# A four-layer vision kernel on one core: the next image's last quarter in the place of the gates' indicators, and letters of their own for setup and tail

## The chip, the core and the metric

The kernel runs on one core of one Trainium2 chip. A core has five engines with instruction streams of their own: TensorE (PE; PEld is its weight load), VectorE (DVE), ScalarE (ACT), GpSimd (POOL) and SyncE (SP), which here only issues DMAs. The metric is the device time in microseconds (us), the median of several runs. Times of single instructions come from one profiled execution.

## The reference

The input x is 8 images of 256 channels and 64 x 64 pixels in float32. Four layers follow each other, each as x + f(groupnorm(x)) with 32 groups:

```
layer 0: b1 = x * sigmoid(bn(conv7x7(max, mean of x over H)))  # maps over (channel, column)
         b2 = the same over W (channel, row); b3 = the same over channels (row, column)
         wts = softmax over the three branches of conv1d(channel means of (b1 + b2 + b3) / 3)
         out = wts[0]*b1 + wts[1]*b2 + wts[2]*b3
layer 1: w = a[0]*weight + sum_i a[i+1] * circulant(weight, b), b = 2, 4, 8, 16; a = softmax(alphas)
         out = conv3x3(x, w)
layer 2: out = x * sigmoid(W2 relu(W1 mean(dwt_ll(x))))          # squeeze and excitation
layer 3: windows of 8 x 8, shifted by 4; qkv = x @ w_qkv + b; 8 heads of 32
         out = softmax(q k^T / sqrt(32) + bias + mask) v @ w_o + b_o
```

## The kernel before, in words

An image has 2 tiles of 128 channels (t or co) by 4096 pixels, held in X. A unit is a half image of one tile, 128 x 2048 values (1 MB); units 0 to 3 go by half, then tile. Layers 0 to 2 are the "front" of an image, in named steps: norm0a to c, reduce0 to 15, zpool, hwconv to hwmean7 (the three gates' maps), logits, mix, mixturn, gate0 to 17, norm1a to c, lift0 to 3 (the first rows of the Winograd form of the convolution), conv0.0 to conv23.1, convend. Each unit's result after layer 2 is stored to scratch_x in DRAM. Layer 3 works on window rows, 64 in all (8 per image), one image behind the front, reading scratch_x.

The order on each engine is written out by hand. The front is the "main line" (letter M); everything else is a stream with a letter. FIRST says which letters are executed after which step of image 0, TURN the same for each later image, AHEAD where they may run ahead, LAST_ROWS the letters after the last front. `play` walks main line and letters and takes the next piece of a stream for each letter. Engines execute in this order and wait on semaphores. The letters that matter here are, on SP, L (load a window row) and S (store it); on POOL, R (row and column sums of the next image), D and W (convolution and DWT work), N (the normalisation of the softmax, L856), O (the lower halves of the heads' output); on ACT, K (tokens), Q (evacuations of a filled bank), X (exponentials, L1129, eight instructions of 64 columns for a unit of 512 scores), T (turned probabilities, L1136), O (heads); on DVE, C (group statistics of the next image, L1615), U (its maxima, L1630), V (row sums for the DWT), J (joined rows), S (bias and maximum, L1724 and L1735), T (totals), A (addition of the attention); on PE, Q (fills: products for q, k, v and the output), S (scores), T (turns), W (weighings with the values).

All fills go through one PSUM bank, QP. A fill waits until the one before it has been read.

The setup (circulant weights, their Winograd halves, the scaling of w_qkv and w_o, the bias tables) stands on the main line: load, alpha and bands ahead of image 0, and the rest after the steps that SETUP_AT names. ScalarE issues sixteen DMAs for w_conv before its first computation.

The next image arrives in X during the convolution: unit u is fetched when its x2 is stored and the DWT has used it, so the fourth is fetched after convend. The gates of layer 0 need, for each pixel, a value that depends on its column and one that depends on its row, both by channel. They are made by TensorE as ab (the values, 64 columns and 64 rows on the 128 partitions) times `ind`, 128 x 4096 indicators of 0 and 1 (L185 and following). `ind` lies behind the tables of the 7 x 7 filters in l0c, and since the convolution uses all of l0c for its waves, tables and indicators are loaded again for every image.

## Time and profile before

| | us |
|---|---|
| median of 3 runs (lowest, highest) | 2962.48 (2961.73, 2963.66) |
| the profiled execution | 2961.15 |
| its span in the profile | 2959.0 |
| image 0 up to its convolution's end | 379.3 |
| its boundary to the first transposes of image 1 | 63.6 |
| a steady image (image 5, 1715.7 to 2043.3) | 327.6 |
| the last eight window rows (from 2698.8) | 260.2 |

The stretches are cut where the last matmul of a convolution ends. Busy time is of the engine alone, and an engine that is busy is not always what the others wait for. PEclk is the granted clock of TensorE as a share of full speed.

### The profile page before, as it was taken

The numbers are of one execution on the slowest core, as the hardware profiler recorded it, in microseconds if no ns is written. First come the engines' busy times: TensorE is split into PE (matmuls) and PEld (weight loads), VectorE is DVE, ScalarE is ACT, GpSimd is POOL, SyncE is SP. The second block draws the span as 40 slices with busy tenths as digits, with TensorE's granted clock in tenths as the row PEclk, the third lists the DMA queues.
The fourth block names the chain that finished last, engine by engine and source line by source line (L and its number), as shares of the span: only waits on it lengthen the run. The fifth ranks groups of instructions, "written<-read, shape, count | busy, mean of one in ns | idle before, by whom it ended". The sixth has DMA issues, their size and how long they took to land.

```text
span 2959.0 us, 68446 instructions
## 1 busy us (share of the span) xinstructions
PE 2369.5 (80%) x27236; PEld 1319.3 (45%) x27236; DVE 2293.1 (77%) x4555; ACT 1707.6 (58%) x4440; POOL 1383.2 (47%) x1052
## 2 busy tenths in 40 slices
PE   0157728899698978899798978898898979898776
PEld 0132315544454545444454545444544545454443
DVE  6868675878787887878887887888887888886443
ACT  0231118655766558654875567654876567655776
POOL 4304471365724574455634573356534572364222
PEclk9977859999899989999899989999999989999998
DMA  5400040004110240005100330005010421011101
GB/s 157 118 3 10 34 149 16 30 30 150 60 37 23 80 143 30 30 30 167 49 31 23 116 107 31 30 30 186 31 44 21 139 72 45 23 51 58 44 30 37
DMA packets 91347, 184.51 MB, mean 62 GB/s; under 512 B 37510, under 2 KB 50454, under 8 KB 80406
## 3 DMA queue, kind: packets, MB, share of 16 engines
q1 hardware_dynamic: 88854, 177.78, 18.5%
q8 instruction: 216, 3.54, 0.5%
q10 hardware_dynamic: 2176, 2.36, 0.3%
q14 instruction: 101, 0.83, 0.1%
HBM read 107.23 MB, written 72.86 MB: 61 GB/s over the span
## 4 chain that ended last, share of the span: by engine, by line
PE 52%; DVE 22%; ACT 11%; issue 7%; POOL 5%; ACTq 1%; SPq 0%; DMA 0%; DVEq 0%; POOLq 0%
PE F L1950 21%; PE QP L2006 6%; PE QP L2022 4%; PE QP L2013 4%; PE SP L2038 3%; PE O L2066 2%; ACT xs L1129 2%; PE PTR L2048 2%; PE F L1828 2%; PE F L1852 1%; ACT g_raw L1011 1%; DVE Z L1630 1%; DVE xs L1748 1%; ACT tmp L968 1%; ACTq L927 1%
## 5 line engine op out<-in xcount | busy, mean ns | idle before, releaser
L1950 PE MATMUL F<-g_raw,cw_hi 128*128 128x512 f16 x2304 | 701.6, 387 | 35.9 <-ACT tmp L1000 23.3
L856 POOL TENSOR_TENSOR xs<-xs,rec 128x512 f32<-128x512 f32 x256 | 283.2, 1107 | 754.2 <-DVE rec L1740 752.3
L1129 ACT ACTIVATE xs<-xs,mx 128x64 f32<-128x64 f32 x2048 | 511.3, 336 | 89.0 <-DVE mx L1735 88.9
L1950 PE MATMUL F<-g_raw,cw_lo 128*128 128x512 f16 x1152 | 443.9, 385 | 0.0
L1950 PEld LDWEIGHTS F<-g_raw,cw_hi 128*128 128x128 f16 x2304 | 220.8, 99 | 293.9 <-ACT tmp L1000 26.9
L1724 DVE TENSOR_TENSOR xs<-SP,bias 128x512 f32<-128x512 f32 (+2 forms) x384 | 181.6, 500 | 112.4 <-PE SP L2038 111.2
L841 POOL TENSOR_TENSOR tmp<-X,uw 128x512 f32<-128x512 f32 x128 | 175.6, 1384 | 186.2 <-DVE X L1587 172.2
L2006 PE MATMUL QP<-tok_hi,qkv_hi 128*128 128x512 f16 x512 | 199.1, 389 | 75.8 <-ACT qq L1114 24.1
L1739 DVE TENSOR_REDUCE sums<-xs 128x8 f32<-128x512 f32 x256 | 173.5, 678 | 94.9 <-ACT xs L1129 93.9
L1852 PE MATMUL F<-ident,g_raw 128*128 128x128 f32 x512 | 102.7, 318 | 156.1 <-ACT tmp L968 143.4
L1327 DVE SCALAR_TENSOR_TENSOR g_raw<-l0c,gn,g_raw 128x512 f16<-128x512 f32 x192 | 177.1, 967 | 52.2 <-ACT g_raw L990 36.3
L865 POOL TENSOR_TENSOR ot_lo<-ot,ot_hi 128x512 f16<-128x512 f32 x128 | 151.9, 1207 | 115.2 <-ACT ot_hi L1150 102.0
L1136 ACT ACTIVATE prt<-PTR 128x512 f32<-128x512 f32 x256 | 150.4, 587 | 90.3 <-PE PTR L2048 89.4
L1630 DVE TENSOR_REDUCE Z<-X 128x16 f32<-128x1024 f32 x128 | 197.7, 1556 | 2.8 <-DMA X<-in_x 2.8
L2006 PE MATMUL QP<-tok_lo,qkv_hi 128*128 128x512 f16 x512 | 197.2, 385 | 0.0
L2006 PE MATMUL QP<-tok_hi,qkv_lo 128*128 128x512 f16 x512 | 197.1, 385 | 0.0
L1748 DVE SCALAR_TENSOR_TENSOR xs<-QP,wm,xs 128x480 f32<-128x480 f32 (+1 forms) x256 | 111.7, 478 | 97.3 <-PE QP L2022 96.8
L2066 PE MATMUL O<-prt,vv 64*32 64x64 f32 x8192 | 167.4, 222 | 23.1 <-ACT prt L1136 22.3
L1117 ACT ACTIVATE kk<-QP,bq,gm 128x512 f32<-128x512 f32 x128 | 99.4, 777 | 148.3 <-PE QP L2006 148.3
L1735 DVE TENSOR_REDUCE mx<-xs 128x8 f32<-128x512 f32 x256 | 175.7, 686 | 8.8
L1114 ACT ACTIVATE qq<-QP,q_bias,q_scale 128x512 f32<-128x512 f32 x128 | 99.3, 776 | 141.5 <-PE QP L2006 141.5
L2048 PE MATMUL PTR<-ident,xs 128*128 128x128 f32 x1024 | 166.3, 287 | 16.5 <-POOL xs L856 12.3
(288 smaller groups left out, 5652.1 us busy)
## 6 DMA issues: line engine op xcount, KB each, us to landing
X<-in_x SPq DMA_DIRECT2D x32, 1024.0 KB, 6.2
scratch_x<-X SPq DMA_DIRECT2D x32, 1024.0 KB, 5.2
xs<-scratch_x SPq DMA_DIRECT2D x56, 512.0 KB, 3.6
out_x<-xs SPq DMA_DIRECT2D x56, 512.0 KB, 2.7
l0c<-scratch_t SPq DMA_DIRECT2D x8, 1876.0 KB, 10.5
l0c<-in_c_ind SPq DMA_DIRECT2D x8, 1024.0 KB, 6.3
l0c<-scratch_t SPq DMA_DIRECT2D x8, 640.0 KB, 12.7
l0c<-scratch_t SPq DMA_DIRECT2D x8, 576.0 KB, 13.2
```

The costliest lines, as they stand in the source:

```text
L841: G.tensor_tensor(rows_view(tmp[:, 2 + m % 2, :]), rows_view(X[:, co, lo:lo + CHUNK]), uw[:, :].unsqueeze(1).to_broadcast([P, ROWS, W]), A ...
L856: G.tensor_tensor(keyed(sc[:, u % 4, :]), keyed(sc[:, u % 4, :]), rec[:, u % 4, :].unsqueeze(2).to_broadcast([P, 8, TOK]), ALU.mult).then_ ...
L1129: last = S.activation(keys, keys, ACT.Exp, bias=mx[:, u % 4, i:i + 1])
L1327: V.scalar_tensor_tensor(vin[:, slot(half, comp), 1, t, :, 1:1 + W], rows_view(src[:, t, :]), g_r[:, t:t + 1], vin[:, slot(half, comp), 0, ...
L1630: V.tensor_reduce(Zv[:, t, kind, 0, PAD + W // 4 * i:PAD + W // 4 * (i + 1)], view[:, part, :], AX.X, ALU.max).then_inc(max_set, 1)
L1724: return V.tensor_tensor(sc[:, buf, :].rearrange("p (g w m) -> p g w m", g=CT, w=4)[:, :, span, :], SP[:, hs, :].rearrange("p (g w m) -> p ...
L1735: V.tensor_reduce(mx[:, buf, :], keyed(sc[:, buf, :]), AX.X, ALU.max, negate=True).then_inc(s_max, 1)
L1739: seq.link(V.tensor_reduce(sums[:, u % 4, :], keyed(sc[:, u % 4, :]), AX.X, ALU.add))
L1950: last = T.matmul(F[:, n % 2, :], wgt[:, ci, C3 * comp + dx, P * co:P * co + P], win[which], start=(ci == 0 and dx == 0 and j == 0), stop= ...
L2006: last = T.matmul(QP[:, :], wgt[:, ci, P * oc:P * oc + P], tk[:, ci, :], start=(j == 0), stop=(j == 5))
L2048: last = T.transpose(PTR[:, P * b:P * b + P], sc[:, u % 4, P * b:P * b + P], ident[:, :])
L2066: last = T.matmul(O[DH * (h % 4):DH * (h % 4) + DH, par, cols:cols + TOK], vv[rows, pair, DH * h:DH * h + DH], prt[rows, u % 2, P * b + TO ...
```

## The change

- **Gates.** `ind` is replaced by `eyes`, two identities of 64 columns one above the other (128 x 64). ab is computed twice, on both halves of the partitions, so that the upper half carries the high halves of the float16 split and the lower half the remainders. A chunk of eight rows takes three matmuls as before; the column part reads `eyes` broadcast over rows, the row part reads eight of its columns, each broadcast over 64. Four transposes instead of two bring ab into place.
- **Early quarter.** The 8 KB per partition that are free in l0c are `quad`: unit 3 of the next image is fetched there as soon as the waves of the convolution have been used (v_lo). The other three go to X as before. `given` tells each reader where a unit lies. Units arrive in the order 0, 3, 1, 2, and statistics and maxima are taken in this order. Gate step 9 writes image data into the place of unit 3 in X, and waits for its store and its use.
- **Maxima and sums by halves.** Column maxima are taken for each half and joined by one instruction. GpSimd's sums over rows are split in halves for their first three additions.
- **Setup.** It has the letter Y on each engine, with more and smaller pieces. w_conv is loaded by SP with eight DMAs of 16 partitions; the circulant weights are stored with eight instead of sixteen.
- **SyncE.** Stores of x2, fetches and constants are the letters Z, F and G.
- **Tail.** In the last eight window rows fills go round three banks, QP and the two of F. Values are taken out of the bank by DVE (P). POOL subtracts the maxima from a unit of scores (X, a 128 x 512 addition) and ACT takes one exponential over 512 columns.
- All tables of letters are other ones, and so is where every stream stands.

```diff
 FIRST = {
-    "SP": {"convend": "L"},
+    "SP": {"reduce0": "Y", "reduce11": "Y", "hwgate": "Y", "band1": "Z", "band2": "YF", "hwmean3": "Z",
+        "conv10.0": "G", "conv13.0": "F", "conv14.0": "F", "conv15.0": "Z", "conv22.1": "F", "convend": "ZL"},
...
 LAST_ROWS = {
-    "POOL": "ENONNNONNNNONNNNNONNNNONNNNNONNNNONNNONNNNNONNO",
+    "POOL": "ENEONNNNXOXNXNXNXNNXONXNXNXXNONXNXXNXNXONXNNXXNXXNONNXXNONXNXNXXNOXNNXXNXNXOXNNNO",
...
-        ind = l0c[:, n_toep + n_hw + n_1d:].bitcast(fp16)
+        quad = l0c[:, n_toep + n_hw + n_1d:]
...
+        def given(img, t, half):
+
+            if img and (half, t) == (1, CT - 1):
+                return quad
+            return X[:, t, HW // 2 * half:HW // 2 * half + HW // 2]
+
+        ARRIVAL = (0, 3, 1, 2)
...
+        ENDING = ROWS_ALL - NW
+        ALONE = FILL[f"q0.{ENDING}"]
+        BY_DVE = [name for name in FILLS if name[0] == "p" or name[0] == "v" and int(name.split(".")[1]) >= ENDING]
...
+        def bank(n):
+
+            return QP[:, :] if n < ALONE or (n - ALONE) % 3 == 0 else F[:, (n - ALONE) % 3 - 1, :]
...
+                    for g in range(P // BMAX):
+                        sp.dma_start(WB[g::P // BMAX, :].rearrange("p (r n) -> p r n", r=BMAX),
+                                     dram(w_conv, g * 2 * BMAX * TAPS, [[BMAX * C * TAPS, BMAX], [C * TAPS, BMAX],
+                                                                        [1, 2 * BMAX * TAPS]])).then_inc(wconv_in, 16)
...
-                            sp.dma_start(ind, c_ind).then_inc(l0c_in, 16)
...
+                def fetches():
+                    for img in range(NB - 1):
+                        at = of_image(img)
+                        for u in ARRIVAL:
+                            half, co, ty, px = unit(u)
+                            if (half, co) == (1, CT - 1):
+                                sp.wait_ge(v_lo, at(v_lo, CT * 2 * COMPS))
+                                sp.dma_start(quad, x[img + 1, P * co:P * co + P, px]).then_inc(x_in[u], 16)
+                            else:
+                                sp.wait_ge(x2_stored[u], 16 * (img + 1))
+                                sp.wait_ge(dwt_used, at(dwt_used, 4 * (u + 1)))
+                                sp.dma_start(X[:, co, px], x[img + 1, P * co:P * co + P, px]).then_inc(x_in[u], 16)
+                            yield u
...
+                def centre(u):
+                    pool.wait_ge(s_max, u + 1)
+                    G.tensor_tensor(keyed(sc[:, u % 4, :]), keyed(sc[:, u % 4, :]),
+                                    mx[:, u % 4, :].unsqueeze(2).to_broadcast([P, 8, TOK]),
+                                    ALU.add).then_inc(s_centred, 1)
...
-                    for q in range(C // BMAX):
-                        act.dma_start(WB[8 * q:8 * q + 8, :].rearrange("p (r n) -> p r n", r=BMAX),
...
                 def exponential(u):
+                    if u >= 4 * ENDING:
+                        act.wait_ge(s_centred, u - 4 * ENDING + 1)
+                        S.activation(sc[:, u % 4, :], sc[:, u % 4, :], ACT.Exp).then_inc(p_exp, 1)
+                        return
...
-                            T.matmul(F[:, n % 2, :], ab_hi[:, P * t:P * t + P], ind[:, px], start=True, stop=False)
-                            T.matmul(F[:, n % 2, :], ab_lo[:, P * t:P * t + P], ind[:, px], start=False, stop=False)
+                            T.matmul(F[:, n % 2, :], ab16[:, P * t:P * t + P],
+                                     eyes[:, :].unsqueeze(1).to_broadcast([P, ROWS, W]), start=True, stop=False)
+                            T.matmul(F[:, n % 2, :], ab16[:, C + P * t:C + P * t + P],
+                                     eyes[:, ROWS * k:ROWS * k + ROWS].unsqueeze(2).to_broadcast([P, ROWS, W]),
+                                     start=False, stop=False)
```

What moves shows in the order of the instructions. First, VectorE at the start of the program, before (L1615 and L1664 are the group statistics, L1337 and following image 0's first norm, L1228 and L1269 the own share of the weights, L1200 and L1229 the first step of a circulant block).

```order
15 L1337 TENSOR_TENSOR gn<-mv,F 128x2
16 L1338 TENSOR_TENSOR F<-mv,F 128x2
17 L1339 TENSOR_TENSOR F<-gn,F 128x2
18 L1340 TENSOR_TENSOR gn<-mv,F 128x2
19 L1341 COPY gn<-F 128x2
20 L1343 COPY m<-F 128x2
21 L1630 TENSOR_REDUCE Z<-X 128x16
22 L1347 TENSOR_SCALAR gn<-F 128x2
23 L1354 SCALAR_TENSOR_TENSOR gn<-F,gn 128x2
24 L1228 TENSOR_SCALAR cw_hi<-xs,al 128x4608
25 L1200 COPY cw_lo<-xs 128x2304
26 L1202 TENSOR_TENSOR cw_lo<-cw_lo,xs 128x128x9
```

and after:

```order
6 L1664 BN_STATS stats<-X 128x6 x2
7 L1679 TENSOR_REDUCE Z<-X 128x16
8 L1664 BN_STATS stats<-X 128x6 x9
9 L1679 TENSOR_REDUCE Z<-X 128x16
10 L1664 BN_STATS stats<-X 128x6 x2
11 L1686 TENSOR_REDUCE Z<-X 128x32
12 L1269 TENSOR_SCALAR cw_hi<-xs,al 128x4608
13 L1229 COPY cw_lo<-xs 128x2304
14 L1232 TENSOR_TENSOR cw_lo<-cw_lo,xs 128x128x9
15 L1233 TENSOR_TENSOR cw_lo<-cw_lo,xs 128x128x9
16 L1238 TENSOR_SCALAR cw_lo<-cw_lo,al 128x128x9 x2
```

The own share and the first block stand ahead of the statistics' aggregation now, and further blocks follow with statistics between them.

Second, VectorE after the end of a steady image's convolution, from a pair of scores to the aggregation of the next image's statistics (L1303, now L1345), before:

```order
1872 L1615 BN_STATS stats<-X 128x6 x2
1873 L1642 TENSOR_TENSOR part<-part,F 128x2
1874 L1643 TENSOR_TENSOR F<-part,F 128x2
1875 L1644 TENSOR_TENSOR F<-part,F 128x2
1876 L1645 TENSOR_TENSOR part<-part,F 128x2
1877 L1739 TENSOR_REDUCE sums<-xs 128x8
1878 L1740 RECIPROCAL rec<-sums 128x8
1879 L1650 TENSOR_SCALAR part<-F 128x2
1880 L1615 BN_STATS stats<-X 128x6 x4
1881 L1303 BN_AGGR mv<-stats 128x2 x2
```

and after:

```order
1905 L1664 BN_STATS stats<-X 128x6
1906 L1698 TENSOR_TENSOR part<-part,F 128x2
1907 L1699 TENSOR_TENSOR F<-part,F 128x2
1908 L1700 TENSOR_TENSOR F<-part,F 128x2
1909 L1701 TENSOR_TENSOR part<-part,F 128x2
1910 L1780 TENSOR_TENSOR xs<-SP,bias 128x512
1911 L1791 TENSOR_REDUCE mx<-xs 128x8
1912 L1706 TENSOR_SCALAR part<-F 128x2
1913 L1664 BN_STATS stats<-X 128x6
1914 L1345 BN_AGGR mv<-stats 128x2 x2
```

The four statistics in one row right before the aggregation have become one, with one more five rows ahead.

Third, what stands in VectorE's last quarter of the convolution now: the statistics of the quarter in l0c and of the X units, a row sum (L1653), and the evacuation of the convolution's banks (L1453, L1454).

```order
1848 L1664 BN_STATS stats<-l0c 128x6
1849 L1664 BN_STATS stats<-X 128x6 x2
1850 L1765 TENSOR_TENSOR tok_lo<-tok,tok_hi 128x512
1851 L1653 TENSOR_REDUCE y<-tmp 128x8
1852 L1804 SCALAR_TENSOR_TENSOR xs<-QP,wm,xs 128x8x60
1853 L1804 SCALAR_TENSOR_TENSOR xs<-QP,wm,xs 128x8x4
1854 L1808 MEMSET sm 128x2
1855 L1664 BN_STATS stats<-X 128x6 x2
1856 L1679 TENSOR_REDUCE Z<-X 128x16
1857 L1453 SCALAR_TENSOR_TENSOR raw<-F,gm,tmp 128x512
```

Before, eight of the sixteen statistics of an image stood within the convolution's steps and eight behind its end; now thirteen stand within and three behind.

Fourth, SyncE from the last part of a steady convolution to the first window row of the next image (L637 and L671 store a unit, L643 and L685 fetch one, L625 to L660 and L648 to L651 are the tables), before:

```order
82 L637 DMA scratch_x<-X 128x2048
83 L680 DMA out_x<-xs 128x2x512
84 L673 DMA xs<-scratch_x 128x2x256 x2
85 L643 DMA X<-in_x 128x2048
86 L637 DMA scratch_x<-X 128x2048
87 L625 DMA l0c<-scratch_t 128x3752
88 L626 DMA l0c<-scratch_t 128x20x64
89 L628 DMA l0c<-scratch_t 128x1152
90 L660 DMA l0c<-in_c_ind 128x4096
91 L643 DMA X<-in_x 128x2048
92 L637 DMA scratch_x<-X 128x2048
93 L643 DMA X<-in_x 128x2048
```

and after:

```order
81 L707 DMA out_x<-xs 128x2x512
82 L685 DMA X<-in_x 128x2048
83 L681 DMA l0c<-in_x 128x2048
84 L700 DMA xs<-scratch_x 128x2x256 x2
85 L671 DMA scratch_x<-X 128x2048
86 L685 DMA X<-in_x 128x2048
87 L671 DMA scratch_x<-X 128x2048
88 L685 DMA X<-in_x 128x2048
89 L648 DMA l0c<-scratch_t 128x3752
90 L649 DMA l0c<-scratch_t 128x20x64
91 L651 DMA l0c<-scratch_t 128x1152
92 L671 DMA scratch_x<-X 128x2048
```

The fetch to l0c (L681) stands ahead of the tables and of the second and third fetch to X, where the fourth fetch stood behind them all (row 93), and the load of the indicators (L660) is gone.

Fifth, ScalarE in the tail, before (L1129 is the exponential, L1114 to L1121 take fills out of the bank):

```order
1787 L1136 ACTIVATE prt<-PTR 128x512
1788 L1129 ACTIVATE xs<-xs,mx 128x64 x8
1789 L1117 ACTIVATE kk<-QP,bq,gm 128x512 x2
1790 L1104 ACTIVATE xs<-xs,coef 128x512
1791 L1136 ACTIVATE prt<-PTR 128x512
1792 L1129 ACTIVATE xs<-xs,mx 128x64 x8
1793 L1121 ACTIVATE vv<-QP 128x512
1794 L1129 ACTIVATE xs<-xs,mx 128x64 x8
1795 L1121 ACTIVATE vv<-QP 128x512
```

and after (L1153 is the exponential):

```order
1788 L1165 ACTIVATE prt<-PTR 128x512
1789 L1153 ACTIVATE xs<-xs 128x512
1790 L1129 ACTIVATE xs<-xs,coef 128x512
1791 L1139 ACTIVATE qq<-QP,q_bias,q_scale 128x512
1792 L1139 ACTIVATE qq<-F,q_bias,q_scale 128x512
1793 L1153 ACTIVATE xs<-xs 128x512
1794 L1142 ACTIVATE kk<-F,bq,gm 128x512
1795 L1165 ACTIVATE prt<-PTR 128x512
1796 L1142 ACTIVATE kk<-QP,bq,gm 128x512
1797 L1165 ACTIVATE prt<-PTR 128x512
```

Eight exponentials of 64 columns have become one of 512, and fills lie in F as well as in QP. GpSimd in the same place now (L885 centres, L879 normalises):

```order
800 L879 TENSOR_TENSOR xs<-xs,rec 128x512
801 L885 TENSOR_TENSOR xs<-xs,mx 128x512
802 L879 TENSOR_TENSOR xs<-xs,rec 128x512
803 L885 TENSOR_TENSOR xs<-xs,mx 128x512
804 L894 TENSOR_TENSOR ot_lo<-ot,ot_hi 128x8x8x8 x2
805 L879 TENSOR_TENSOR xs<-xs,rec 128x512
806 L885 TENSOR_TENSOR xs<-xs,mx 128x512
807 L879 TENSOR_TENSOR xs<-xs,rec 128x512 x2
```

A centring stands between the normalisations, where before there were only these and L865.

## Rows read from the trace of the kernel before

**Rows 1.** The page, section 1: busy time of each engine over the span.
```profile
PE 2369.5 (80%) x27236; PEld 1319.3 (45%) x27236; DVE 2293.1 (77%) x4555; ACT 1707.6 (58%) x4440; POOL 1383.2 (47%) x1052
```

**Rows 2.** Busy time by stretch: stretch, length, engines (instructions), clock, DMA share, GB/s.
```profile
44.60:117.40 72.80, 2.25 (x8) 1.68 (x8) 69.17 (x161) 2.38 (x2) 16.30 (x12) 1.00 0.25 60
...
151.00:253.20 102.20, 57.82 (x265) 29.58 (x265) 74.25 (x189) 23.45 (x69) 12.54 (x10) 0.68 0.03 2
253.20:379.30 126.10, 101.43 (x440) 44.37 (x440) 92.49 (x137) 20.33 (x32) 59.67 (x40) 0.88 0.13 47
379.30:442.90 63.60, 7.33 (x27) 5.05 (x27) 47.87 (x90) 7.28 (x11) 47.43 (x37) 0.52 0.37 130
...
1715.70:2043.30 327.60, 289.64 (x3401) 162.19 (x3400) 272.22 (x536) 210.69 (x548) 170.48 (x129) 0.96 0.20 66
...
2698.80:2959.00 260.20, 187.44 (x3156) 112.56 (x3154) 121.77 (x287) 186.06 (x487) 68.36 (x64) 0.92 0.13 44
```

**Rows 3.** The same of image 5: its first stage and its convolution.
```profile
1715.70:1740.20 24.50, 15.24 (x256) 9.89 (x254) 21.86 (x59) 12.17 (x30) 18.95 (x16) 0.87 0.57 174
...
1905.10:2043.30 138.20, 134.22 (x1121) 66.58 (x1115) 112.46 (x173) 73.50 (x176) 77.99 (x55) 0.99 0.26 85
```

**Rows 4.** Timeline of the start: start, us, engine, line, operation, count, idle before.
```profile
3.56 36.14 ACTq L927 DMA_DIRECT2D xs<-in_w_conv  x10
...
22.06 0.51 SPq L571 DMA_DIRECT2D tok_lo<-in_c_mask  x1
...
41.27 0.16 DVE L1222 TENSOR_REDUCE sm<-al 128x1 f32<-128x5 f32 x1 [17.21 <-ACT al L933]
...
48.11 2.61 DVE L1228 TENSOR_SCALAR cw_hi<-xs,al 128x4608 f32<-128x4608 f32 x1
...
107.64 5.19 SPq L601 DMA_DIRECT2D scratch_w<-cw_hi  x4
111.06 4.95 DVE L1238 TENSOR_REDUCE gm<-cw_hi 128x1 f32<-128x4608 f32 x1
...
117.39 0.75 DVE L1432 TENSOR_REDUCE Z<-F 128x1 f32<-128x256 f32 x2
```

**Rows 5.** Timeline, TensorE in image 0's convolution.
```profile
317.50 1.03 PE L1950 MATMUL F<-g_raw,cw_hi 128*128 128x512 f16 x2 [18.79 <-ACT tmp L1000]
```

**Rows 6.** Timeline, VectorE after the end of image 5's convolution.
```profile
2045.96 1.21 DVE L1630 TENSOR_REDUCE Z<-X 128x16 f32<-128x1024 f32 x1
...
2064.72 2.46 DVE L1615 BATCH_NORM_STATS2 stats<-X 128x6 f32<-128x512 f32 x4
```

**Rows 7.** The page, section 6: DMA issues, KB each, median us to landing.
```profile
X<-in_x SPq DMA_DIRECT2D x32, 1024.0 KB, 6.2
...
l0c<-scratch_t SPq DMA_DIRECT2D x8, 576.0 KB, 13.2
```

**Rows 8.** Busy time of the tail, 2730 to 2959 us, and its groups by line.
```profile
2730.00:2959.00 229.00, 164.43 (x2770) 97.74 (x2767) 99.25 (x218) 167.12 (x443) 55.73 (x52) 0.92 0.12 41
...
L1129 ACT ACTIVATE xs<-xs,mx 128x64 f32<-128x64 f32 x268 | 67.0, 335 | 8.7 <-DVE mx L1735 8.6
L856 POOL TENSOR_TENSOR xs<-xs,rec 128x512 f32<-128x512 f32 x34 | 35.4, 1043 | 144.2 <-DVE rec L1740 144.2
L2006 PE MATMUL QP<-tok_hi,qkv_lo 128*128 128x512 f16 x64 | 24.3, 379 | 0.0
...
L1735 DVE TENSOR_REDUCE mx<-xs 128x8 f32<-128x512 f32 x33 | 22.6, 686 | 1.1
...
L1136 ACT ACTIVATE prt<-PTR 128x512 f32<-128x512 f32 x34 | 19.9, 585 | 8.4 <-PE PTR L2048 8.3
...
L2013 PEld LDWEIGHTS QP<-qkv_hi,tok_hi 128*128 128x128 f16 x64 | 7.1, 111 | 12.9 <-ACT vv L1121 10.2 <-ACT kk L1117 0.7
...
L2006 PEld LDWEIGHTS QP<-tok_hi,qkv_hi 128*128 128x128 f16 x62 | 6.0, 97 | 34.3 <-ACT qq L1114 14.3 <-DVE xs L1748 7.2 <-ACT kk L1117 6.3
...
L2022 PEld LDWEIGHTS QP<-ot_hi,wo_hi 128*128 128x128 f16 x36 | 3.7, 103 | 19.4 <-ACT vv L1121 9.9 <-DVE xs L1748 4.2 <-issue 3.5
```

360 lines of the change are left out of this document (187 added, 173 removed), and 126 rows, old and new, of tables (FIRST, TURN).

## The prediction, on record before the changed kernel ran

> **What bounds the kernel now.** I read the page first, then the busy time of each engine stage by stage, then the start, the boundary between two images and the tail by timeline and by groups. TensorE is busy 80% of the span, VectorE 77% [rows 1]: two engines near full on average, so what counts is where each of them waits. By stage there are four regimes [rows 2]. (1) Setup, 44.6 to 117.4: VectorE works 69.2 of 72.8 us on the convolution's circulant weights while TensorE has 2.3 us. (2) Image 0 has no attention beside it: 151.0 to 253.2 keeps VectorE busy 74.3 of 102.2 and TensorE 57.8 (clock 0.68), and the boundary after it, 379.3 to 442.9, is VectorE 47.9 and GpSimd 47.4 of 63.6, TensorE 7.3. (3) A steady image takes 327.6 us with TensorE at 289.6; its convolution is TensorE's (134.2 of 138.2), its first 24.5 us are VectorE's (21.9) [rows 3]. Images 2 to 7 are alike, so any per-image term counts about 7 times. (4) The tail, 260.2 us, has no engine full: ScalarE 186.1, TensorE 187.4, VectorE 121.8.
>
> **The change, part by part.** All sums are made against the profiled execution (2961.15 us; its span is 2959.0). The median of the runs, 2962.48, lies 1.3 higher, and I add that at the end.
>
> *Setup and image 0.* Before, ScalarE issues the sixteen loads of the weights until 39.7 us and only then computes the exponentials that VectorE waits for (17.21 us idle at 41.27) [rows 4]. VectorE starts on the circulant part at 48.11, after image 0's norm, and the first reduction stands at 117.39, behind 4.95 us of peak. Now SyncE issues eight loads after its constants, from about 22.6 us (the last constant's issue begins at 22.06), ScalarE is free at once, and VectorE's order has the circulant part ahead of the norm (the first order fences). How long do eight loads take? The nearest row is the store of the same bytes in sixteen pieces, 22.49 us of issue [rows 4]. If a piece with twice the partitions lasts twice as long, the weights are there at 22.6+22.5+3, about 48, and only the peak's 4.95 us leave the path; if it lasts as long as now, they are there at 22.6+11.2+3, about 37, which adds 11 to 12 us. The piece that lasts as long as now would make the first reduction some 17 us earlier; the bounds are 5 and 19. I take 17, since the loads of the images (1 MB, 6.2 us to landing, [rows 7]) show that the queues carry far more than these pieces ask.
>
> The Trainium skill ("DMA: Bandwidth & Descriptors", the section on why a DMA increments its semaphore by 16) says that a transfer is split over as many of 16 engines as divide its slow dimensions, so that a piece of 8 partitions uses 8 engines and one of 16 all. By that rule a piece of twice the partitions takes no longer, and the loads would be there at 37; no row before holds a piece of 16 partitions to test it by, only the sixteen of 8, at 22.49 us for 2.4 MB.
>
> From 117.4 to 253.2 the setup's six turns stand serially on the main line, now they are pieces between the reductions and the bands. VectorE's busy 74.3 of 102.2 us is the floor, so at most 28 us are there, and I take 17 (0 if the pieces only move the waits). In the convolution of image 0 TensorE stands 18.79 us behind one block that scales the attention's weights and waits for GpSimd [rows 5]. Split into pieces early in the image, this goes but for about 5 us: 14. The boundary after image 0 is bound by GpSimd's sums, which are the same: 2. Together 17+17+14+2 = 50, from 25 to 65.
>
> *The last quarter fetched early, per steady image.* Before, the fourth unit's fetch waits for the last x2 and VectorE executes 8 statistics of the next image after the convolution's end; the last four, 2.46 us, stand right before the norm [rows 6]. The new order leaves 3 and 8 row sums instead of 9, against one longer maximum (0.7 us more): 5 x 0.63 + 0.68 - 0.7 = 3.1 us less. Nothing is late in their place at once: the fetch of the last unit takes 6.2 us and was there already. At the end of the reduction stage three maxima and a total stand now before the pooling, then one maximum and a 0.2 us combination: 2 less. The doubled matrix of the gate's weights costs two more transposes (under 0.38 each, which a matmul of four times the columns takes in [rows 8]), a twice as wide copy on ScalarE and small work on VectorE: 1.3 more, on the path. The gate's three matmuls per chunk keep their columns: nothing, while stride-0 reading costs nothing extra (TensorE is full there, so 16 chunks x 2 x 0.05 us, 1.6, is the price if it does; I leave 0). The maxima are still sixteen per image; 6 more GpSimd sums per image lie beside idle time (170.5 busy of 327.6). The 1 MB of indicators is replaced by a 1 MB quarter, so traffic falls by 1 MB an image, off the path.
>
> Against this stands the convolution. TensorE has 4 us of idle there [rows 3], and by the letters of the two tables it is given 23 fills for 20, 5 scores for 4, 9 weighings for 10: three fills are 18 matmuls x 0.38 [rows 8] = 6.9 more, with the other letters and turns 4.4 net. VectorE gets 13 statistics there for 8, from 112.5 busy of 138.2: covered, unless they wait. What leaves the other stages pays only where TensorE is full there: 1. So per image -3.1 -2 +1.3 -1 +4.4 = -0.4; I round it to -1, for the DVE work that leaves the short stages, and carry -9 (VectorE's whole removal and nothing paid in the convolution) to +5.7 (4.4 + 1.3 and no gain). Seven times: -7.
>
> *The tail.* Between 2730 and 2959 TensorE is busy 164.4 of 229.0 us, ScalarE 167.1 [rows 8]. TensorE's fills share one bank and wait 34.3 + 12.9 + 19.4 us before their weight loads; of that 52.8 us have the bank's readers as named releaser. With three banks this is free to go. ScalarE loses the eight exponentials of each unit: 268 instructions, 67.0 us, become 33.5 of 512 elements at 0.585 (the row of the same width), 19.6, so 47 less, and 9.4 of value copies go to VectorE (99.3+10). GpSimd gets 32 x 1.04 (its normalisation's row has the same shape), 33 to 55.7, so 89 of 229. After that the longest is TensorE's 164.4. Its dependence chain from row to row has one more link, GpSimd's 1.04 us in front of the exponential, against 2.0 - 0.6 us saved in it. Of the 52.8 us I take two thirds, 35, since a part will show as a wait for tokens or for the clock (0.92 here); bounds 0 and 53.
>
> The Trainium skill ("GPSIMD Engine Reference", section 4.1, Engine selection) speaks against the centring on GpSimd, as it calls VectorE about twice as fast on elementwise work with two inputs. The trace agrees in part: 1.04 us for the shape there against 0.69 for as many elements on VectorE (L1735) [rows 8]. As ScalarE pays 2.0 us per unit now, this costs nothing unless GpSimd, at 89 of 229 us, becomes late.
>
> Sum: -50 -7 -35 = -92 of 2961.15 is 2869; with 1.3 for the median, 2870.
>
> **Rivals.** *R1, little of it arrives.* Setup gives 38 and the tail half, 17: the wait for the single bank turns into one for normalised rows (L856 has 144.2 us of idle behind VectorE's totals, so the chain of score, maximum, exponential, total, normalisation is long already). The images give 0. 2962.5-55 = 2907. For it: no engine is full in the tail, so a chain rules. Against: a bank released by four different engines in turn is what stands in front of the weight loads. *R2, the images give more.* All of VectorE's removal in the waiting stages, 7 x -7 rather than -1 each: 2870-42 = 2828. For it: the first stage of an image has TensorE idle for 9.3 of 24.5 us [rows 3]. Against: the convolution's 4 us of slack. *R3, slower.* In the steady convolution the next image's statistics stand in VectorE's order behind transfers. The second half of the order has the second unit's statistics 12.8 us of VectorE's own work behind the row sum that releases its fetch, and the last one's 6.2 us behind (third pair of fences); with 13.2 us to landing, as the slowest of the table loads has [rows 7], in place of 6.2, VectorE stands for up to 7.4 us in the convolution, with the gathering of TensorE's banks queued behind it. With 5.7 us that makes 13.1 x 7 = 92, against 85 gained elsewhere: 2969. It decides above 12.1 us per image, and 6.2 is what every fetch shows. *R4, nothing*: the order changes cancel, 2962.
>
> **Chances.** Forecast 0.60, R1 0.20, R2 0.12, R3 0.05, R4 0.03. The likeliest case's own range is 2845 to 2900. The range that holds 8 in 10 goes to R1 and to R2: 2825 to 2922. A change of 0.2%, 6 us, is what can be told here. Faster 0.91 (forecast, R1, R2 less 0.01), same 0.03, slower 0.06.
>
> **What would show it.** Right if the first reduction is near 100 us; if the stall of 18.8 us before TensorE in image 0's convolution is gone; if a steady image takes 325 to 329 us with the convolution 138 to 143 and the first stage near 21; if the tail is about 225 with its ScalarE near 130 busy and no long wait of fills for a bank. Wrong in its largest terms if the eight loads end after 45 us, if GpSimd's centring shows as the releaser of ScalarE's exponentials for more than 20 us, or if images differ from 327.6 by over 3 us in either sense, which the sevenfold count makes the greatest risk. VectorE waiting for an X load within the convolution would show R3.

## The result, and the profile after

The changed kernel takes 2877.85 us in the median of four runs (2871.03 to 2880.82), the kernel before 2962.11; the ratio is 0.971 (95% interval 0.9695 to 0.9725), 84 us less. Forecast were 2870, and 2825 to 2922 as the range. The profiled execution is the fastest of the four, 2871.03 with a span of 2869.2, 89.8 less than the span of before. One execution of the variant t2 below took 5854.68 us, with no cause on record, and is left out of its median.

The same stretches as [rows 2], cut where the last matmul of a convolution ends; columns as there.

```profile
135.80:229.50 93.70, 58.31 (x267) 32.08 (x268) 70.75 (x187) 23.77 (x69) 17.70 (x14) 0.65 0.00 1
229.50:354.80 125.30, 106.27 (x432) 44.03 (x432) 99.85 (x139) 20.68 (x32) 59.23 (x41) 0.91 0.24 77
354.80:411.30 56.50, 4.78 (x20) 4.12 (x20) 44.40 (x89) 5.86 (x9) 46.95 (x42) 0.53 0.16 56
...
1679.60:2003.60 324.00, 287.11 (x3402) 163.07 (x3401) 271.39 (x538) 210.00 (x548) 168.17 (x135) 0.97 0.19 63
2652.50:2869.20 216.70, 179.63 (x3157) 111.85 (x3154) 131.35 (x304) 135.41 (x248) 101.99 (x96) 0.94 0.16 53
```

Image 0 ends at 354.8 instead of 379.3. Its boundary to image 1's transposes takes 56.5 us in place of 63.6, but image 1 then takes 4.0 more, so that the first two images gain 27.6. Images 2 to 7 take 1951.3 together in place of 1970.0, 18.7 less in this execution, and the tail 216.7 in place of 260.2. 24.5 + 3.1 + 18.7 + 43.5 = 89.8. The third of these terms is the least certain one: in nine profiles of kernels with these images (this one, and those of a_again, i1, s2, s3, t1, t2, t4 and v1 below) images 2 to 7 take 1951.3 to 1966.4, 3.6 to 18.7 less than before, and this profile is the lowest. The tail is steadier: in the seven profiles that have it unchanged (six of these nine, and q1) it takes 214.6 to 217.9.

The start, as [rows 4] (timeline: start, us, engine, line, operation):

```profile
12.89 5.27 SPq L597 DMA_DIRECT2D xs<-in_w_conv  x8
...
28.07 2.62 DVE L1269 TENSOR_SCALAR cw_hi<-xs,al 128x4608 f32<-128x4608 f32 x1 [5.25 <-DMA xs<-in_w_conv]
...
94.44 4.95 DVE L1275 TENSOR_REDUCE gm<-cw_hi 128x1 f32<-128x4608 f32 x1
99.31 0.74 DVE L1474 TENSOR_REDUCE Z<-F 128x1 f32<-128x256 f32 x2
```

Eight loads are issued in 5.27 us and VectorE takes the own share at 28.07, 20.0 earlier than before; the first reduction of image 0 stands at 99.31, 18.1 earlier. SyncE was at the weights at 12.9 and not at 22.6: without ScalarE's sixteen loads beside it, its own small constants go out faster (with eight beside it, in s3 below, they end at about 15.9).

### The profile page after: what moved, and what is told of

Read it like the earlier page. It is cut to its first block and busy times, and to the rows that moved or that the text cites. A ratio compares the mean times of both kernels' runs of the same rounds, so it can differ in the third digit from the quotient of the medians.

```text
span 2869.2 us, 68252 instructions
## 1 busy us (share of the span) xinstructions
PE 2368.1 (83%) x27252; PEld 1337.8 (47%) x27252; DVE 2303.8 (80%) x4579; ACT 1654.8 (58%) x4200; POOL 1390.7 (48%) x1132
## 5 line engine op out<-in xcount | busy, mean ns | idle before, releaser
L879 POOL TENSOR_TENSOR xs<-xs,rec 128x512 f32<-128x512 f32 x256 | 282.0, 1102 | 731.4 <-DVE rec L1796 728.5
L1158 ACT ACTIVATE xs<-xs,mx 128x64 f32<-128x64 f32 x1792 | 447.4, 336 | 131.4 <-DVE mx L1791 131.4
L2021 PEld LDWEIGHTS F<-g_raw,cw_hi 128*128 128x128 f16 x2304 | 222.6, 99 | 296.4 <-issue 19.6
L2080 PE MATMUL QP<-tok_hi,qkv_hi 128*128 128x512 f16 x470 | 182.8, 389 | 51.9 <-ACT qq L1139 28.9
L1369 DVE SCALAR_TENSOR_TENSOR g_raw<-l0c,gn,g_raw 128x512 f16<-128x512 f32 x192 | 171.2, 934 | 50.0 <-ACT g_raw L1016 35.2
L2140 PE MATMUL O<-prt,vv 64*32 64x64 f32 x8192 | 175.0, 228 | 32.1 <-ACT prt L1165 28.3
L2122 PE MATMUL PTR<-ident,xs 128*128 128x128 f32 x1024 | 170.0, 291 | 32.1 <-POOL xs L879 18.1
L2080 PE MATMUL QP<-tok_hi,qkv_lo 128*128 128x512 f16 x470 | 181.2, 385 | 0.0
L2080 PE MATMUL QP<-tok_lo,qkv_hi 128*128 128x512 f16 x470 | 181.0, 385 | 0.0
L1139 ACT ACTIVATE qq<-QP,q_bias,q_scale 128x512 f32<-128x512 f32 x118 | 91.5, 775 | 153.7 <-PE QP L2080 153.2
L2021 PEld LDWEIGHTS F<-g_raw,cw_lo 128*128 128x128 f16 x1152 | 113.7, 99 | 141.7 <-issue 5.6
L2140 PEld LDWEIGHTS O<-prt,vv 64*32 64x32 f32 x8192 | 133.2, 112 | 88.8 <-issue 46.2
L2112 PE MATMUL SP<-kk,qq 32*64 32x64 f32 x8192 | 155.7, 226 | 14.9 <-ACT kk L1142 10.2
```

What stands on the lines that cost most here:

```text
L879: G.tensor_tensor(keyed(sc[:, u % 4, :]), keyed(sc[:, u % 4, :]), rec[:, u % 4, :].unsqueeze(2).to_broadcast([P, 8, TOK]), ALU.mult).then_ ...
L1158: last = S.activation(keys, keys, ACT.Exp, bias=mx[:, u % 4, i:i + 1])
L1369: V.scalar_tensor_tensor(vin[:, slot(half, comp), 1, t, :, 1:1 + W], rows_view(src[:, t, :]), g_r[:, t:t + 1], vin[:, slot(half, comp), 0, ...
L2021: last = T.matmul(F[:, n % 2, :], wgt[:, ci, C3 * comp + dx, P * co:P * co + P], win[which], start=(ci == 0 and dx == 0 and j == 0), stop= ...
L2080: last = T.matmul(out_bank, wgt[:, ci, P * oc:P * oc + P], tk[:, ci, :], start=(j == 0), stop=(j == 5))
L2122: last = T.transpose(PTR[:, P * b:P * b + P], sc[:, u % 4, P * b:P * b + P], ident[:, :])
```

## Experiments

Times are medians, and a ratio is that of the means; where two kernels are compared by stage, it is by their profiles, with the same cuts.

**The tail: the banks alone, in the kernel before** (b1_banks)

```diff
+        def bank(n):
+            return QP[:, :] if n < ALONE or (n - ALONE) % 3 == 0 else F[:, (n - ALONE) % 3 - 1, :]
...
-                        pe.wait_ge(qp_read, FILL[name])
+                    if FILL[name] > ALONE + 2:
+                        wait_read(pe, FILLS[FILL[name] - 3])
```

> The kernel before with one thing of the change, the three banks of the tail; order, values on ScalarE and eight exponentials as before. Its tail is 260.2 us, of which 52.8 us are waits of fills for the bank. Theory A: 20 to 35 us less. Theory B, ScalarE at 186 busy and the order hold the tail: under 8 us less, since each wait for the bank turns into one for an exponential or a copy.

2948.21 us against 2962.65, ratio 0.9956 (0.9942 to 0.997); the tail takes 245.8 in place of 260.2. 14.4 us lie between the two theories. The fills hardly wait for their bank any more, and TensorE waits for normalised scores in their place, 25.6 us before weight loads where it was 10.2 (the first row is of the kernel before, in the same window from 2700 us to the end):

```profile
PEld PTR L2048 <- POOL xs L856: 10.2, 13, 2.4
...
PEld PTR L2063 <- POOL xs L868: 25.6, 19, 2.6
PE PTR L2063 <- POOL xs L868: 17.4, 16, 2.4
```

(columns: engine and line, what it waited for, us in total, times, longest.) Of 52.8 us of waits only about a quarter was time.

**The tail: without the centring** (t2_eight_exp), **with two banks** (t1_two_banks), **values on ScalarE** (t4_act_values), each in the changed kernel

```diff
# t2: centre() issues nothing, and
-                    if u >= 4 * ENDING:
-                        act.wait_ge(s_centred, u - 4 * ENDING + 1)
-                        S.activation(sc[:, u % 4, :], sc[:, u % 4, :], ACT.Exp).then_inc(p_exp, 1)
-                        return
# t1
-            return QP[:, :] if n < ALONE or (n - ALONE) % 3 == 0 else F[:, (n - ALONE) % 3 - 1, :]
+            return QP[:, :] if n < ALONE or (n - ALONE) % 2 == 0 else F[:, 0, :]
# t4
-        BY_DVE = [name for name in FILLS if name[0] == "p" or name[0] == "v" and int(name.split(".")[1]) >= ENDING]
+        BY_DVE = [name for name in FILLS if name[0] == "p"]
```

> The changed kernel without the centring on GpSimd: eight exponentials of 64 columns with the maximum as bias for each unit of the tail, as before. ScalarE's busy time in the tail goes from 135 of 217 us to about 180, GpSimd's from 102 to 69. Theory A, banks first: the banks gave most of the 43.5 us, so this costs 5 to 10 us. Theory B, ScalarE was as much a bound as the bank: 180 busy of 217 is as full as before, and 20 us or more of the 43.5 come back.

> The changed kernel with two banks for the fills of the tail (QP and one half of F) in place of three, all else the same. Its tail is 216.7 us. Theory A, the waits for the bank were what the tail lost: with two banks a fill waits again for the reader of the fill two before it, and the tail grows by 5 to 12 us. Rival, the chain of score, exponential and normalisation sets the tail: under 2 us more, since a second bank is already one more than the chain needs.

> The changed kernel with the sixteen evacuations of values in the tail done by ScalarE, as before, each pair just ahead of the turned probabilities of its row's first unit; VectorE leaves them out. Three banks, centring on GpSimd and one exponential stay. So far the kernel before gave 14.4 us with the banks alone, and the changed one loses 15.7 to 17.8 us of its tail without the centring, which leaves some 12 of 43.5 us to the values and the order. Theory A, the values matter little: ScalarE goes from 135 to 145 of 217 us busy, which is no bound; the tail grows by under 4 us and the 12 us belong to the order. Rival, VectorE's values shorten the chain of a row: 6 to 12 us more.

The tail of t2, then of t1 and of t4 (columns as in [rows 2]; the changed kernel's row stands above):

```profile
2663.10:2895.50 232.40, 183.82 (x3156) 114.86 (x3154) 131.19 (x304) 177.38 (x472) 69.33 (x64) 0.91 0.15 49
```

```profile
2658.80:2881.40 222.60, 183.57 (x3157) 112.75 (x3154) 131.88 (x304) 135.69 (x248) 102.31 (x96) 0.92 0.15 52
```

```profile
2658.70:2878.30 219.60, 178.52 (x3157) 112.67 (x3154) 123.44 (x288) 142.81 (x264) 102.91 (x96) 0.94 0.15 52
```

Without the centring the tail is 15.7 us longer (232.4) and the time 2900.54, 23 above the changed kernel's 2877.85 and 19 above its later 2881.49; ScalarE is at 177.4 busy of 232.4 again. That is between the two theories, nearer to the second. The third bank is worth 5.9 us (222.6), 4.7 by the longest of the seven unchanged tails (217.9), and its time, 2884.11, is 6 above the first median and 3 above the second, as theory A said. The values on VectorE are worth 2.9 (219.6) by the first profile, but only 1.7 by the longest of the seven, and its time of 2881.55 equals the changed kernel's 2881.49 on another chip (a_again, below). So of 43.5 us the banks alone give 14 and the centring some 16. About 13 are left, of which the values have 2 to 5; the rest comes only with the new order or with the parts together, and which of the two was not tried apart.

The centring has the price that was read for it (1.06 us for 1.04), and ScalarE's single exponential nearly so (0.62 for 0.585). ScalarE waits 15.3 us for centred scores, under the 20 that the prediction named as a sign of being wrong:

```profile
L879 POOL TENSOR_TENSOR xs<-xs,rec 128x512 f32<-128x512 f32 x35 | 37.1, 1065 | 39.0 <-DVE rec L1796 39.0
L885 POOL TENSOR_TENSOR xs<-xs,mx 128x512 f32<-128x512 f32 x32 | 33.8, 1056 | 40.3 <-DVE mx L1791 40.0
...
L1153 ACT ACTIVATE xs<-xs 128x512 f32<-128x512 f32 x32 | 19.8, 623 | 15.4 <-POOL xs L885 15.3
```

**The start: eight loads alone, in the kernel before** (b4_loads)

```diff
-                    for q in range(C // BMAX):
-                        act.dma_start(WB[8 * q:8 * q + 8, :].rearrange("p (r n) -> p r n", r=BMAX), ...
+                    for g in range(P // BMAX):
+                        sp.dma_start(WB[g::P // BMAX, :].rearrange("p (r n) -> p r n", r=BMAX), ...
```

> The kernel before with one thing of the change, w_conv loaded by SyncE in eight pieces behind its constants; order as before. The own share on VectorE began at 48.11 us there and at 28.07 in the changed kernel. Theory: all of the start's gain but the peak's place comes from this, the first reduction moves from 117.39 to 98 to 102 us, and the time falls by 15 to 19 us. Rival: VectorE's statistics and norm, which stand ahead of the circulant part in this order, and the later setup take most of it back: under 8 us.

2944.73 against 2962.65, ratio 0.9948 (0.9931 to 0.9964). The first reduction stands at 99.10 and image 0 ends at 360.6. The theory holds: 18 of the 84 us are these eight DMAs. (Two of its ten executions took 2959, so that the means differ by 15 only; the spans of the profiles differ by 18.5.) VectorE has its old order here, with the statistics and the norm ahead of the circulant part, and the first reduction stands where the changed kernel has it, at 99.31: the new order adds nothing up to there.

**Sixteen pieces from SyncE** (s2_sp_sixteen) **and eight from ScalarE** (s3_act_eight), in the changed kernel

```diff
# s2
-                    for g in range(P // BMAX):
-                        sp.dma_start(WB[g::P // BMAX, :].rearrange("p (r n) -> p r n", r=BMAX), ...
+                    for q in range(C // BMAX):
+                        sp.dma_start(WB[8 * q:8 * q + 8, :].rearrange("p (r n) -> p r n", r=BMAX), ...
# s3: the same loop over g, taken from SyncE's load() to the head of ScalarE's
-                        sp.dma_start(WB[g::P // BMAX, :].rearrange("p (r n) -> p r n", r=BMAX), ...
+                        act.dma_start(WB[g::P // BMAX, :].rearrange("p (r n) -> p r n", r=BMAX), ...
```

> The changed kernel with w_conv loaded by SyncE at the same place in the old sixteen pieces of 8 partitions, in place of eight of 16. Eight pieces were issued in 5.27 us and the own share began at 28.07. Theory A, a piece of 8 partitions uses half of the DMA engines (the rule of the Trainium skill's DMA: Bandwidth & Descriptors by which the slowest dimension sets them): the load takes about 10 us longer, the first reduction comes 8 to 12 us later, and so does the end. Rival, only the engine that issues and the place behind the images mattered: under 3 us.

> The changed kernel with the eight loads of w_conv issued by ScalarE at its start, in place of SyncE behind the constants. With sixteen pieces by SyncE the own share began at 51.6 us, with eight at 28.07. Theory A, the size of the pieces decides: eight pieces from ScalarE are there by 20 to 27 us, beside the images' loads, ScalarE's exponentials wait until about 10 us, and the time is the changed kernel's less 0 to 6 us. Rival, the engine decides: ScalarE's issue is stretched over 20 us or more, as its sixteen were over 39, and the own share begins at 35 us or later, 7 us or more slower.

Timeline rows of s2, and the stretch in which the weights are under way (columns as in [rows 2]; the DMA share and GB/s are the last two):

```profile
12.89 20.78 SPq L597 DMA_DIRECT2D xs<-in_w_conv  x16
...
51.60 2.62 DVE L1270 TENSOR_SCALAR cw_hi<-xs,al 128x4608 f32<-128x4608 f32 x1 [28.82 <-DMA xs<-in_w_conv]
...
18.00:35.00 17.00, 0.00 (x0) 0.00 (x0) 4.78 (x6) 0.00 (x0) 1.86 (x6) 1.00 0.55 68
```

the same stretch of the changed kernel:

```profile
18.00:23.00 5.00, 0.00 (x0) 0.00 (x0) 4.81 (x6) 0.00 (x0) 2.06 (x8) 1.00 1.09 210
```

and of s3:

```profile
0.74 13.30 ACTq L958 DMA_DIRECT2D xs<-in_w_conv  x8
...
15.60 0.16 DVE L1264 TENSOR_REDUCE sm<-al 128x1 f32<-128x5 f32 x1 [9.50 <-ACT al L965]
...
28.65 2.61 DVE L1269 TENSOR_SCALAR cw_hi<-xs,al 128x4608 f32<-128x4608 f32 x1
```

Sixteen pieces take 20.78 us to issue at the place where eight take 5.27, and VectorE stands 28.82 us for them: the own share begins 23.5 us later, and the time is 2900.4, 22.6 above the changed kernel's first median and 19 above its second. Theory A was right in the cause and too small by half: from the first issue to the own share it is 38.7 us against 15.2, more than twice. The rows of the stretch show two parts in this. The DMA engines' busy share is 0.55 in s2 and 1.09 in the changed kernel (over 1 since packets overlap on an engine), half as much; and each byte holds an engine about 1.6 times as long in s2 (0.55 for 68 GB/s against 1.09 for 210). The rule that a DMA spreads over as many engines as divide its slowest dimensions (the Trainium skill, "DMA: Bandwidth & Descriptors", section Why a DMA increments its semaphore by 16 and not by 1) agrees with the halved share, though no row names the engines; by its factor of two alone the load would have ended near 43 and not 51.6. Why a byte takes longer in s2 is open.

With eight from ScalarE the own share begins at 28.65, and the time is 2881.69 against 2881.49 on the same chip. VectorE does not wait for the weights there: it has stood 9.50 us for ScalarE's exponential behind the 13.30 us of issue, and executes statistics and maxima from 16.9 to 28.65, so that the row says only that the weights were there by then. The engine that issues made no difference to the time, the form of the pieces did. The two forms differ in two ways that no run took apart: in the partitions covered (8 against 16), and in which these are (neighbours in s2, every eighth in the changed kernel).

**The early quarter taken back** (q1_late_quarter; the statistics' letters of VectorE move with it)

```diff
-        ARRIVAL = (0, 3, 1, 2)
+        ARRIVAL = (0, 1, 2, 3)
...
-        "conv7.0": "L", "conv7.1": "S", "conv8.1": "F", "conv15.0": "F", "conv15.1": "L", "conv16.0": "Z",
-        "conv16.1": "FZ", "conv18.1": "F", "conv21.0": "G", "conv21.1": "Z", "conv23.1": "S"},
+        "conv7.0": "L", "conv7.1": "S", "conv8.1": "F", "conv15.1": "L", "conv16.0": "Z",
+        "conv16.1": "FZ", "conv18.1": "F", "conv21.0": "G", "conv21.1": "ZF", "conv23.1": "S"},
```

> The changed kernel with the next image's unit 3 fetched last, behind the store of the last x2, and read last: units arrive as 0, 1, 2, 3, the four statistics of the quarter that stood within the convolution stand right before the image's norm. Theory A, VectorE's work in the first stage of an image is what the early quarter takes away: four statistics of 0.63 us and some waiting, 2.5 to 4 us per image in the first stage, 17 to 28 us in seven images. Rival, the convolution gets back what the first stage loses, since TensorE is full there and VectorE loses work in it: under 7 us in all.

2902.02 against 2961.12, ratio 0.9791 (0.9775 to 0.9807): 24 us above the changed kernel's first median and 20.5 above its second, 3.4 or 2.9 for each of seven images. The four statistics of the quarter stand in one row right before the norm again, and the first stage of image 5 takes 26.0 us:

```profile
1692.00:1718.00 26.00, 19.63 (x321) 13.71 (x318) 21.75 (x57) 12.20 (x29) 18.22 (x15) 0.80 0.61 197
```

```profile
1714.87 2.45 DVE L1664 BATCH_NORM_STATS2 stats<-l0c 128x6 f32<-128x512 f32 x4
```

The convolution is 139.8 us with and without, so nothing is paid back. Theory A. It is not quite the stage of before: that took 24.5 us [rows 3], 1.5 less than here, so the quarter's worth is that within the new order.

**The changed code in the order of before** (o1_old_order)

```diff
-        ARRIVAL = (0, 3, 1, 2)
+        ARRIVAL = (0, 1, 3, 2)
...
+"SP": {... "conv6.0": "Z", "conv11.0": "F", "conv12.0": "Z", "conv17.0": "F", "conv18.0": "Z", "conv20.0": "GF", "conv23.0": "F", ...
```

The other tables are those of before, with the letters Y of the setup in blocks at the steps that SETUP_AT named; the tail has one bank and eight exponentials.

> The changed kernel's code (identities in place of the indicators, doubled matrix, early quarter, maxima and sums by halves, eight loads and eight stores) in the order of the kernel before: its tables, its setup on the main line in one block per step, units arriving in the order 0, 1, 3, 2, one bank and eight exponentials in the tail. Theory A, the code alone gives nothing in an image and the order gives it: image 0 near 360 us as with the eight loads alone, steady images 327.6 plus about 1.3 for the doubled matrix, tail 260; total 2946 to 2956. Rival, the early quarter and the maxima by halves pay by themselves: images of 325 and a total under 2935.

2938.03 against 2961.12, ratio 0.9921 (0.9907 to 0.9936), 6.7 below b4_loads. A steady image takes what it took before:

```profile
1688.10:2015.80 327.70, 288.60 (x3404) 162.15 (x3403) 272.69 (x537) 210.78 (x548) 171.22 (x135) 0.96 0.19 63
```

The doubled matrix costs 0.5 us between the channel means and the first gate (13.5 in place of 13.0), not 1.3, and the gate stage is 32.0 against 31.9. The total is lower than theory A said (2946 to 2956), because image 0 (357.9) and image 1 (346.6 for 349.4) gain a little too and the 1.3 per image are not there; its statement that the code alone gives nothing in a steady image holds.

**Two letters moved in image 0** (i1_move_setup)

```diff
-    "conv0.1": "Y", "conv2.0": "D", "conv3.0": "DD",
+    "conv2.0": "D", "conv3.0": "DDY",
...
-    "conv10.0": "BBVVY",
+    "conv10.0": "BBVV", "conv10.1": "Y",
```

> The changed kernel with two letters moved in image 0's convolution: GpSimd's two all-reduces for the scales of the attention's weights stand after its lower differences of step conv3.0 instead of after conv0.1, and VectorE's second scaling piece of conv10.0 after conv10.1. In the changed kernel TensorE has five waits of 3.2 to 4.0 us in this convolution, the third (at 265.0) behind an evacuation that waits 13.4 us for GpSimd, the fourth (at 295.4) behind the scaling piece. Theory A, the single stall of 18.8 us came back as these, because pieces stand ahead of evacuations: both waits go, with the slow matmuls behind each, 6 to 10 us in image 0. Rival, image 0's convolution is held by VectorE's and GpSimd's total work, and the waits come back elsewhere in it: under 2 us.

2878.87 against the changed kernel's 2877.85 elsewhere; by the profile, image 0's convolution takes 122.8 us in place of 125.3. Only one of the two moves came about. GpSimd's all-reduces begin at 270.08 in place of 252.91, but VectorE executes the same instructions in the same order as in the changed kernel, with the scaling piece (here from 292.44) still right in front of the evacuation (294.86). So this run tests the wait behind GpSimd alone. That one is gone: the evacuation waits for TensorE now, and four of the five waits are left, 4.89, 2.54, 5.30 and 3.83 us, 16.6 together for 18.0. A gain of 2.5 us is nearer to the rival than to theory A. What the scaling piece costs in its place no run shows.

**The weights ahead of the constants** (v1_weights_first), **and the changed kernel again on the same chip** (a_again)

```diff
+                    for g in range(P // BMAX):
+                        sp.dma_start(WB[g::P // BMAX, :] ...).then_inc(wconv_in, 16)
                     for dst, src in small:
                         sp.dma_start(dst, src).then_inc(consts_in, 16)
-                    for g in range(P // BMAX):
-                        sp.dma_start(WB[g::P // BMAX, :] ...).then_inc(wconv_in, 16)
```

> The changed kernel with the two letters moved as in i1_move_setup and SyncE's eight loads of w_conv ahead of the twelve constants. VectorE waited 5.25 us for these weights before 28.07. Theory A: the own share starts 3 to 5 us earlier, the first reduction with it, and with the 2.5 us of the moved letters the time is 2870 to 2874, 4 to 8 us below the changed kernel. Rival: the weights share the queues with 4 MB of images that are ahead of them, so they land no earlier than about 27 us, and later constants hold up ScalarE's or GpSimd's setup: within 3 us of the changed kernel.

> The changed kernel once more, on the chip of the two above. Its images 2 to 7 took 324.0 to 327.8 us in the first profile, and in the profiles of five variants with the same images 323.7 to 328.5. Theory A, the granted clock in the first 60 us of an image sets which: an image with TensorE at 0.85 or more in the first stage and 0.92 or more in the reductions takes 324 to 325 us, one with 0.78 and 0.88 takes 327 to 328.5, and the median is near 2878. Rival: the 324 us of the first profile are this kernel's own, and the variants' edits cost the 3 us.

v1 takes 2872.47 (2869.12 to 2876.78), a_again 2881.49 (2880.4 to 2883.57): v1 is the fastest kernel of this study, 9 us below the changed one beside it. Its own share starts at 26.40, 1.7 earlier and not 3 to 5 as theory A had it, and with the letters of i1 image 0 ends at 349.4, 5.2 before a_again's 354.6. So 5 of the 9 us have their place; the other 4 are not placed, and images 2 to 7 alone differ by more from one execution to another (1951.3 and 1963.0, below). First stages and reductions of image 6 in the first profile of the changed kernel:

```profile
2003.60:2026.40 22.80, 18.24 (x321) 12.71 (x320) 19.72 (x54) 9.70 (x21) 16.94 (x13) 0.85 0.59 192
...
2039.30:2080.30 41.00, 30.55 (x413) 19.93 (x417) 37.58 (x70) 39.20 (x122) 35.48 (x33) 0.96 0.08 27
```

and in a_again:

```profile
2008.60:2031.60 23.00, 18.31 (x321) 12.37 (x320) 19.41 (x54) 9.88 (x22) 17.31 (x14) 0.85 0.58 191
...
2044.90:2087.80 42.90, 33.14 (x412) 21.38 (x416) 37.91 (x70) 39.40 (x122) 35.13 (x33) 0.88 0.08 26
```

The reductions take 41.0 us at a granted clock of 0.96 and 42.9 at 0.88, with the same instructions. Images 2 to 7 add up to 1951.3 in the first profile and 1963.0 in this one; over nine profiles of kernels with these images single ones lie between 323.7 and 329.1. Theory A holds for the reductions; for the first stage the clock is 0.85 in both. The time of an image goes with the granted clock of the whole image: the thirteen of these 54 with 0.963 or more take 323.7 to 325.6 us, the six with 0.943 take 328.3 to 329.1. So the 324 us are not the first profile's own (t1 and t4 have 323.7 and 324.6 too), but they are its luck: the median came out at 2881.49 and not near 2878.

## Why the prediction was right

The sum was made of three terms, -50, -7 and -35, and the spans gave -27.6, -18.7 and -43.5. The total of -92 against -89.8 (84 by the medians) is right in part by luck: the first term was nearly twice what came, and in this profile the other two were too small.

- *Start, 17.* Measured 18.1 at the first reduction. The choice between bounds was right: eight pieces take no longer each than sixteen do (0.66 us of issue each against 1.30 in s2). The rest of the working was not, and its errors cancel. The load was to begin at 22.6 and the weights to be there at 37; it began at 12.9, and they were there at 28.07, 9 us earlier for a reason that no term had. The peak still stands ahead of the first reduction (94.44, above); only its all-reduce and the scaling moved behind, so its 4.95 us were no part of the gain. And VectorE's new order adds nothing here (b4).
- *Reductions to convolution, 17.* Measured 5.6: this stretch ends 5.6 us less after the first reduction than before (33.6 + 102.2 before, 36.5 + 93.7 now). VectorE is busy 70.8 of 93.7 where it was 74.3 of 102.2, so that 23 of its 28 us of idle time are still there. That these are the small steps' own waits, from one engine to another and back, is likely but was not tried.
- *Convolution of image 0, 14.* Measured 0.8. **This is the step of the sum that failed.** The stall of 18.79 us [rows 5] is gone as forecast, and in the second quarter of this convolution 15.4 us go with it. The quarters before:

```profile
253.20:286.00 32.80, 27.87 (x109) 11.50 (x110) 25.48 (x25) 8.41 (x14) 18.69 (x10) 0.85 0.00 0
286.00:331.00 45.00, 26.21 (x118) 11.96 (x117) 31.80 (x50) 6.49 (x10) 18.47 (x13) 0.77 0.06 24
331.00:355.60 24.60, 23.65 (x109) 10.45 (x108) 19.23 (x40) 4.05 (x6) 9.19 (x8) 1.00 0.24 86
355.60:379.30 23.70, 23.70 (x109) 10.47 (x107) 15.99 (x23) 1.38 (x2) 13.32 (x11) 1.00 0.35 116
```

and after:

```profile
229.50:269.00 39.50, 28.46 (x109) 11.36 (x110) 22.57 (x28) 8.53 (x14) 14.04 (x11) 0.89 0.00 1
269.00:298.60 29.60, 25.70 (x109) 10.69 (x109) 28.26 (x31) 6.72 (x10) 17.63 (x10) 0.94 0.14 39
298.60:328.20 29.60, 25.55 (x108) 10.80 (x108) 24.69 (x39) 4.05 (x6) 12.64 (x9) 0.93 0.29 87
328.20:354.80 26.60, 26.55 (x108) 11.17 (x108) 24.33 (x44) 1.37 (x2) 14.92 (x12) 0.89 0.65 222
```

The other quarters take 6.7, 5.0 and 2.9 us more, 14.6 together. TensorE has five waits in this convolution, of 3.2 to 4.0 us, 18.0 together; with the short ones it stands 19.0 us in place of 24.7 (4.93, 18.79 and 0.95 before). Three of them, and a matmul behind the second of these:

```profile
251.39 0.60 PE L2021 MATMUL F<-g_raw,cw_hi 128*128 128x512 f16 x2 [3.43 <-ACT tmp L1026]
...
268.96 0.84 PE L2021 MATMUL F<-g_raw,cw_hi 128*128 128x512 f16 x2 [3.95 <-DVE ytj L1454]
269.59 0.63 PE L2021 MATMUL F<-g_raw,cw_lo 128*128 128x512 f16 x1
...
298.59 0.60 PE L2021 MATMUL F<-g_raw,cw_hi 128*128 128x512 f16 x2 [3.15 <-DVE ytj L1454]
```

The second of the three comes from GpSimd, where the all-reduces had pushed the first unit's work back so that VectorE's evacuation waits 13.40 us (without them there, in i1, this wait is gone). In front of the third stands a scaling piece of VectorE, ahead of an evacuation (at 297.14); that it is the cause is read from the order and was not tested:

```profile
267.50 0.75 DVE L1453 SCALAR_TENSOR_TENSOR raw<-F,gm,tmp 128x512 f32<-128x512 f32 x1 [13.40 <-POOL X L790]
...
293.76 0.93 DVE L1316 TENSOR_SCALAR prt<-prt,gm 128x768 f32<-128x768 f32 x1
294.72 1.50 DVE L1317 CAST qkv_hi<-prt 128x768 f16<-128x768 f32 x1
296.26 0.96 DVE L1318 TENSOR_TENSOR qkv_lo<-prt,qkv_hi 128x768 f16<-128x768 f32 x1
297.14 0.74 DVE L1453 SCALAR_TENSOR_TENSOR raw<-F,gm,tmp 128x512 f32<-128x512 f32 x1
```

And most waits are paid twice. Behind four of the five, at once or after up to six matmuls at full rate, 8 to 14 matmuls run at half the rate (0.63 us for a single one, as at 269.59, where it is 0.38 otherwise; they follow each other every 0.43 us and not every 0.22). Behind the first, of 3.64 us, none does. The granted clock is at its lower level there, 0.50, as behind the wait that ends at 251.39:

```profile
252.20:255.50 3.30, 3.30 (x10) 1.14 (x8) 1.89 (x4) 0.00 (x0) 0.76 (x2) 0.50 0.00 0
```

By the spacing of this convolution's matmuls 28 ran at the lower rate before and 50 now, six of the 22 more at its very start; 22 x 0.21 = 4.6 us. So of 5.7 us less of waits slow matmuls take 4.6 back, which leaves about 1 (0.8 measured). I had priced the stall by its length and forgot that what had stood in it must be put somewhere, in a stage where both VectorE and TensorE had little room (VectorE is busy 99.9 us of this convolution now, 92.5 before).

- *Boundary after image 0, 2.* It is 7.1 shorter, but the rest of image 1 takes 4.0 more: 3.1.
- *Steady images, -1 each.* Boundary: forecast 3.1 less on VectorE, and a first stage near 21 us. The first stage of image 5 takes 22.6 for 24.5, 1.9 less (23.0 in a_again). The 2.9 to 3.4 per image that q1 takes back are those of the quarter within the new order. Right in kind, and the term of the sum that carries the change's name. The doubled matrix was forecast 1.3 and costs 0.5. The gates' stride-0 reading was put at nothing, rightly; the 0.05 us a matmul named as its price otherwise stand in no row. The convolution was forecast 4.4 longer and is 1.6 longer (139.8 for 138.2). This term was mis-sized in both of its factors. Counted in the traces of image 5, it has one fill of values more, 19 for 18, and not three fills more:

```profile
L2013 PE MATMUL QP<-qkv_hi,tok_hi 128*128 128x256 f16 x16 | 4.4, 273 | 0.0
```

```profile
L2087 PE MATMUL QP<-qkv_hi,tok_hi 128*128 128x256 f16 x20 | 5.5, 273 | 0.0
```

(four of these matmuls make a fill with the eight of its two other groups; before, then after). And a matmul of 512 columns was priced at its length of 0.38, where in a full stream they overlap and follow each other every 0.22. What I had not priced is the moving of letters between other stages: the channel means and logits take 3.3 us more each, the gates 4.1 less, the reductions 3.6 less, the norm 3.0 less. Over images 2 to 7 the first profile gives 18.7, a_again 7.0, forecast was 6: right, within what the clock makes of them.
- *Tail, 35.* Measured 43.5. Right in kind (bounds 0 and 53), but not by its reasoning: two thirds of the bank's 52.8 us of waits were to be the gain, and the banks alone give 14.4. The saving on ScalarE, which I had put down as room and not as time, gives 16. The number came out by luck, since both stood in one term.

The rivals: R1's "half the tail" would have been 17 and R1's wait for normalised scores does appear when the banks stand alone. R3 did not come: the statistics wait 4.2 us for transfers in the whole program, of which 3.8 are one wait at the start, for image 0 (at 14.49).

```profile
L1664 DVE BATCH_NORM_STATS2 stats<-X 128x6 f32<-128x512 f32 x100 | 65.3, 678 | 4.8 <-DMA X<-in_x 4.2
...
L1664 DVE BATCH_NORM_STATS2 stats<-l0c 128x6 f32<-128x512 f32 x28 | 18.4, 679 | 0.0
```

R2's larger gain of images did not come either. The rule that GpSimd is about twice as slow as VectorE on elementwise work with two inputs (the Trainium skill, "GPSIMD Engine Reference", section 4.1, Engine selection) agrees in sign: 1.06 us here, and 0.68 for an addition of the same shape on VectorE (L1724 before, 128 of them). The centring on GpSimd paid all the same, as it relieved ScalarE and GpSimd had room. Whether it would have paid more on VectorE, busy 131.4 of 216.7 us in the tail, was not tried.

## What to carry to other kernels

A stall that is removed by spreading its work is worth its length only if the stages that receive the pieces have room on the engine that does them; look there for evacuations that the pieces would stand in front of, and add what the clock takes behind each new short wait. Waits for one resource in a chain are an upper bound of its worth by far: here 52.8 us of them were 14.4 us. Before moving a load to another engine, ask first how it is cut: how many partitions each piece covers, and which.

## What the runs showed of the hardware that was not expected

- Loads of 8 neighbouring partitions: sixteen take 20.78 us to issue and 38.7 from the first issue to the use, at a DMA share of 0.55. Eight of 16 spread partitions with the same bytes take 5.27 and 15.2 at a share of 1.09. The time of issue depends on what is under way: 6.95 for the same eight in b4, 10.49 right behind the images' loads in v1, 13.30 from ScalarE beside them in s3.
- TensorE's granted clock falls to its lower level of 1.2 GHz behind four of five waits of 3.2 to 4.0 us, and 8 to 14 matmuls of 512 columns run at it before they are back at 2.4; behind one wait of 3.64 us it did not fall. In an image's reductions it makes 2 us of difference (0.96 or 0.88 granted), and the same kernel's executions go with it: 2871.03 at 0.938 on average, 2877.62 to 2880.82 at 0.933 and 0.934.
- A moving operand read by broadcast (stride 0 in rows or in columns) costs TensorE nothing: 385 and 380 ns for 512 columns of `eyes`, against 383 and 379 of the full indicators.

```profile
L1920 PE MATMUL F<-l0c,ab_hi 128*128 128x512 f16 x16 | 6.1, 383 | 0.0
L1921 PE MATMUL F<-l0c,ab_lo 128*128 128x512 f16 x16 | 6.1, 379 | 0.0
```

```profile
L1990 PE MATMUL F<-eyes,ab 128*128 128x512 f16 x16 | 6.1, 380 | 0.0
L1988 PE MATMUL F<-eyes,ab 128*128 128x512 f16 x15 | 5.8, 385 | 0.4 <-DVE X L1561 0.4
```
